# Forget gates of a linear-attention block as a bounded running product, and the last image's attention moved one chunk forward

## The chip, the cores and the metric

One core of one Trainium2 chip runs the whole program in one launch. The metric is the time of one execution on the device in microseconds (us). Before the change the median of three runs is 594.33 us (593.33 to 594.6).

## The reference, cut to what matters

Four images of 512 tokens go through a tokenizer (sines and cosines of six multiples of the input, times a weight matrix), a causal linear attention with forget gates, and a mixture of experts with a shared expert. A class token stands ahead of each image; it is the same for all, so it is computed once. The change touches the forget gates:

```
q = (elu(x @ Wq) + 1) * scale
k = elu(x @ Wk) + 1
v = x @ Wv
forget = sigmoid(x @ Wf + bf)
log_f = log(clip(forget, 1e-06, None))
log_f_cum = clip(cumsum(log_f, axis=1), -20, 20)
exp_neg, exp_pos = exp(-log_f_cum), exp(log_f_cum)
kv = k[..., :, None] * v[..., None, :]
Mstate = exp_pos[..., None] * cumsum(exp_neg[..., None] * kv, axis=1)
z = exp_pos * cumsum(exp_neg * k, axis=1)
h = einsum('blm,blmd->bld', q, Mstate) / (einsum('blm,blm->bl', q, z)[..., None] + 1e-06)
```

D = 192 features, M = 64 attention features, 512 tokens and the class token in a sequence. The kernel weighs q with exp_pos and k with exp_neg, and takes scores as one product of the two, masked by causality.

## The kernel before, in words

Every engine has its own program, written out by hand, and waits on semaphores. TensorE (PE) sets the pace. The program has three stages.

**Token stage** (to about 372 us). For each image b, `project(b, k)` for k = 0 to 8 multiplies nine groups of features into two PSUM banks, 48 PE instructions in the trace for each group. The features of a group come from GpSimd (POOL, L405), VectorE (DVE, `remainders`, L767 and L771) and ScalarE (ACT, `sines`, L476 and L479), in three slots. Between the groups PE does one attention step each of what is ready: beside image 0 the class token (called attention 0), beside image b the attention of image b - 1 (attention b, "a" in the code). The steps are `attn1` (transposes), `attn2` (gate, q, k and the first values), `attn2b` (the other values), `attn3` (scores), `attn5` (scores times values), `attn6`, `attn7` (output projection), `attn8`, `router`, `ranks`.

The gates in `attn2`: ACT takes exp(-x) into tile row R_S (`odds`, L513) and an exponential for q and k (L516). DVE cuts the odds (L805) and adds up q and k (L807). ACT takes ln(1 + odds) (`log_odds`, L521), DVE a running sum over the tokens (`running_sum`, a scan, L813) and a clip (L818), ACT the exponential of plus or minus that (`powers`, L526), DVE the product with q and k (`weigh_qk`, L824). A DMA that ACT's queue issues then moves k from the upper 64 partitions to the lower (`move_k`, L532), and PE's scores wait for it. On ACT sine, exponential, logarithm and SiLU each need their table loaded (ACT_TABLE_LOAD) when another was used before.

**Shared stage** (about 372 to 486 us). No token groups are left; PE fills the time around attention 4, that of the last image (B = 4), with chunks q = 0 to 18 of the shared expert. In chunk q it does `up(q)` (two halves of five matmuls, L1469 to L1473), the attention step that the table of numbers `Q_...` puts at q, and `down(q - 2)` (L1507). ACT does `silu(q)`, DVE `hidden(q)` (L1032), both with the same table for the attention steps behind them. ACT also rounds the expert weights (`expert_hi`, at `Q_HI`), DVE takes the remainders (`expert_lo`, L1056 and L1060, at `Q_LO`). Every sixth `down` begins a new image of the shared expert in the same PSUM banks, so `down(6)` waits for `finish(0)` and `down(12)` for `finish(1)` (L1040), which DVE does in chunk Q_X2 and in chunk Q_RK + 1. `places` is the arithmetic of the tokens' slots, after which GpSimd scatters the tokens.

**Expert stage** (from about 486 us). 39 tiles of gathered tokens go through the routed experts, then the class token's and five more chunks of the shared expert, the sums and the output.

```
Q_X1, Q_QKV, Q_V23, Q_RK3, Q_SCORES, Q_AV, Q_X2, Q_WO, Q_X3, Q_LG, Q_RK = 1, 2, 3, 4, 5, 6, 8, 9, 11, 12, 13
Q_HI = (5, 8, 11, 13)
Q_LO = (6, 9, 12, 14)
```

Of the kernel before, what the change touches and what calls it, by code (L numbers as in the profile page):

```python
# [11 lines left out]
ALU = mybir.AluOpType  # L12
ACT = mybir.ActivationFunctionType
AX_X = mybir.AxisListType.X

P = 128
B = 4
# [5 lines left out]
M = 64  # L23
# [33 lines left out]
MAX_ODDS = float(np.float32(1e6) - np.float32(1.0))  # L57
CLIP = 20.0
FAR = 1e30
# [8 lines left out]

Q_X1, Q_QKV, Q_V23, Q_RK3, Q_SCORES, Q_AV, Q_X2, Q_WO, Q_X3, Q_LG, Q_RK = 1, 2, 3, 4, 5, 6, 8, 9, 11, 12, 13
Q_HI = (5, 8, 11, 13)  # L70
Q_LO = (6, 9, 12, 14)

# [8 lines left out]
def build(nc, xT, wT, freqs, cls_tok, packed, wsa, wsb, wds, wea, web, wdea, wdeb, blank, slots, ydram, out):  # L81
    with ExitStack() as ctx:
        def sb(name, shape, dt=F32):
            return ctx.enter_context(nc.sbuf_tensor(name, shape, dt))
# [39 lines left out]
        f_col = sb("f_col", [P, NF + 3])  # L124
        qk_scale, p_sign = sb("qk_scale", [P, 1]), sb("p_sign", [P, 1])
        half_pi, warm = sb("half_pi", [P, 1]), sb("warm", [P, 1])
        one = sb("one", [P, 1])
# [23 lines left out]
        with ExitStack() as fourth:  # L151
# [9 lines left out]
        s_c = sb("s_c", [P, 1])  # L161
# [26 lines left out]

        R_E, R_PHI, R_S, R_P, R_C, R_QK, R_K = range(7)
        at = r[:, 0:4, :]  # L190
# [4 lines left out]
            h_ready ln_step xn_ready xpose1 xta_ready xtb_ready qk_psum f_psum v01_psum v23_psum v_ready  # L195
            e_ready ee_ready odds_ready oddsc_ready s_ready scan_ready c_ready p_ready phi_ready
            qk_ready k_in at_psum at_diag at_rest state_psum state_ready av_psum den_ready rden_ready hh_ready hn_ready
# [11 lines left out]
         h_ready, ln_step, xn_ready, xpose1, xta_ready, xtb_ready, qk_psum, f_psum, v01_psum, v23_psum, v_ready,  # L209
         e_ready, ee_ready, odds_ready, oddsc_ready, s_ready, scan_ready, c_ready, p_ready, phi_ready,  # L210
         qk_ready, k_in, at_psum, at_diag, at_rest, state_psum, state_ready, av_psum, den_ready, rden_ready, hh_ready, hn_ready,
# [14 lines left out]
        def width(a):  # L226

            cls = a == 0
            return (CLS, CLS, 1) if cls else (T, P, NT)
# [234 lines left out]
        def _(act):  # L464
# [52 lines left out]

            def log_odds(a):
                W, TP, nt = width(a)
                act.wait_ge(oddsc_ready, a + 1)  # L520
                act.activation(r[:, R_S, 0:W], r[:, R_S, 0:W], ACT.Ln, bias=one[:, :], scale=1.0).then_inc(s_ready, 1)  # L521

            def powers(a):
                W, TP, nt = width(a)
                act.wait_ge(c_ready, a + 1)
                act.activation(r[:, R_P, 0:W], r[:, R_C, 0:W], ACT.Exp, scale=p_sign[:, :]).then_inc(p_ready, 1)  # L526

            def move_k(a):
# [5 lines left out]
            def attn2(a):  # L534
                take_v(a, 0)
                odds(a)
                if a >= 1:
                    take_v(a, 1)
                log_odds(a)
                powers(a)  # L540
                move_k(a)
# [109 lines left out]
            for b in range(1, B):  # L651

                sines(b, 1)
                sines(b, 2)
                attn1(b)
                if b >= 2:
                    router(b - 1)
                sines(b, 3)
                odds(b)
                take_v(b, 0)  # L660
                sines(b, 4)
                take_v(b, 1)
                log_odds(b)
                powers(b)
                move_k(b)
                if b >= 2:
                    take_ranks(b - 1)
                sines(b, 5)
                attn3(b)
                sines(b, 6)  # L670
                sines(b, 7)
                attn6(b)
                sines(b, 8)
                attn8(b)
                if b + 1 < B:
                    sines(b + 1, 0)
                take_h(b)


            for q in range(NQB):  # L680
                silu(q)
                if q == Q_X1:
                    router(B - 1)
                    attn1(B)
                if q == Q_QKV:
                    odds(B)
                    take_v(B, 0)
                if q == Q_V23:
                    log_odds(B)
                    take_v(B, 1)  # L690
                    powers(B)
                    move_k(B)
                if q == Q_RK3:
                    take_ranks(B - 1)
                if q == Q_SCORES:
                    attn3(B)
                if q == Q_X2:
                    attn6(B)
                if q == Q_X3:
                    attn8(B)  # L700
                if q == Q_LG:
                    router(B)
                if q == Q_RK:
                    take_ranks(B)
                if q in Q_HI:
                    expert_hi(Q_HI.index(q))

# [16 lines left out]
        def _(dve):  # L724
# [77 lines left out]
            def clip_odds(a):  # L802
                W, TP, nt = width(a)
                dve.wait_ge(odds_ready, a + 1)
                dve.tensor_scalar(r[:, R_S, 0:W], r[:, R_S, 0:W], MAX_ODDS, None, ALU.min).then_inc(oddsc_ready, 1)  # L805
                dve.wait_ge(ee_ready, a + 1)
                dve.scalar_tensor_tensor(r[:, R_PHI, 0:W], ps[:, A2, 0:W], 0.0, r[:, R_E, 0:W],  # L807
                                         ALU.max, ALU.add).then_inc(phi_ready, 1)

            def running_sum(a):  # L810
                W, TP, nt = width(a)
                dve.wait_ge(s_ready, a + 1)
                dve.tensor_tensor_scan(r[:, R_C, 0:W], one[:, 0:1].to_broadcast([P, W]), r[:, R_S, 0:W],  # L813
                                       0.0 if a == 0 else s_c[:, 0:1], ALU.mult, ALU.add).then_inc(scan_ready, 1)
                dve.wait_ge(scan_ready, a + 1)
                if a == 0:
                    dve.tensor_copy(s_c[:, :], r[:, R_S, 0:1])
                dve.tensor_scalar(r[:, R_C, 0:W], r[:, R_C, 0:W], CLIP, -CLIP, ALU.min, ALU.max).then_inc(c_ready, 1)  # L818

# [7 lines left out]
            def attn2(a):  # L827
                negatives(a)
                clip_odds(a)
                running_sum(a)  # L830
                weigh_qk(a)
# [297 lines left out]
            dve.memset(qk_scale[M:P, :], 1.0)  # L1129
            dve.memset(p_sign[0:M, :], -1.0)  # L1130
            dve.memset(p_sign[M:P, :], 1.0)
            for t_ in (cnt, nbk, dold, nxt, emap):
# [36 lines left out]
            for b in range(1, B):  # L1169
# [14 lines left out]
                remainders(b, 4)  # L1184
                running_sum(b)
                weigh_qk(b)
# [20 lines left out]
            for q in range(NQB):  # L1207
# [10 lines left out]
                if q == Q_V23:  # L1218
                    running_sum(B)
                    weigh_qk(B)  # L1220
# [5 lines left out]
                if q == Q_AV:  # L1226
                    places(B - 1, [2])
                if q in Q_LO:
                    expert_lo(Q_LO.index(q))
# [549 lines left out]
```

## Time and profile before

| | |
|---|---|
| runs | 593.33, 594.6, 594.33 us; median 594.33 |
| profiled execution | 599.89 us, its span from first to last instruction 597.7 us |
| granted TensorE clock, mean | 0.975 of full |
| busy | PE 562.9 us (94%), DVE 363.3 (61%), ACT 249.8 (42%), POOL 173.8 (29%) |
| chain that ended last | PE 86%, DVE 8%, ACT 2%, DMA 1%, issue 1% |

Times in the trace count from the first instruction. A row of the timeline has start, duration, engine, line, operation, output and inputs, and in brackets how long the engine had been idle before it and who released it. A matmul in fp32 takes two PE instructions. The granted clock is 1.00 at TensorE's full clock (2.4 GHz) and 0.50 at the lower (1.2 GHz).

### The profile page before, as it was taken

Reading aid. Unit: us, or ns where it says so; the run is one execution under the profiler, and the core shown is the slowest. Engines: PE = TensorE matmul, PEld = TensorE weight load, DVE = VectorE, ACT = ScalarE, POOL = GpSimd, SP = SyncE. Lnnn points to the kernel's source line nnn. Section 1 sums busy time; section 2 is a strip of 40 time slices with the busy share of each in tenths; the row PEclk is TensorE's granted clock in tenths of the full one; section 3 lists DMA queues with packets and bytes.
Section 4 is the critical chain, followed back from the end, with each engine's and each line's share of the span. In section 5 each row is a group of like instructions: output and inputs, shape, how many; then the busy total and the mean of one; then the engine's idle time right before and its main releaser. Section 6 shows DMA issues by size and latency. Waiting matters only on the chain.

```text
span 597.7 us, 9035 instructions
## 1 busy us (share of the span) xinstructions
PE 562.9 (94%) x3247; PEld 516.8 (86%) x3247; DVE 363.3 (61%) x1041; ACT 249.8 (42%) x345; POOL 173.8 (29%) x200
## 2 busy tenths in 40 slices
PE   2999999999999999999999999999688699999996
PEld 2998999889999899999899999678577589999865
DVE  5636787443788627878537773646477436665536
ACT  2455364752423745224754242562223025455410
POOL 5412223131344114644311630005000504444410
PEclk9998999999999999999899999999798799999999
DMA  8900057000100001100000101401000651522173
GB/s 285 330 27 19 1 207 232 19 26 1 36 1 18 19 10 35 63 28 1 0 1 9 54 19 41 172 10 71 1 1 1 203 169 41 157 77 73 54 221 111
DMA packets 23648, 42.48 MB, mean 71 GB/s; under 512 B 2663, under 2 KB 15205, under 8 KB 23509
## 3 DMA queue, kind: packets, MB, share of 16 engines
q1 hardware_dynamic: 19568, 33.31, 17.5%
q0 software_dynamic: 3472, 8.07, 3.8%
q10 hardware_dynamic: 564, 0.53, 0.4%
q8 instruction: 27, 0.44, 0.3%
q14 instruction: 17, 0.13, 0.1%
HBM read 31.73 MB, written 14.79 MB: 78 GB/s over the span
## 4 chain that ended last, share of the span: by engine, by line
PE 86%; DVE 8%; ACT 2%; DMA 1%; issue 1%; POOL 0%; ACTq 0%; DVEq 0%
PE ps L1314 45%; PE ps L1507 5%; PE ps L1393 2%; PE ps L1559 2%; PE ps L1561 2%; PE ps L1469 2%; PE ps L1370 2%; PE ps L1471 2%; PE ps L1470 2%; PE ps L1472 2%; PE ps L1473 1%; PE ps L1342 1%; PE ps L1537 1%; PE ps L1538 1%; PE ps L1541 1%
## 5 line engine op out<-in xcount | busy, mean ns | idle before, releaser
L1314 PE MATMUL ps<-w_tok,feat 128*128 128x192 f32 x1728 | 293.4, 331 | 12.0 <-ACT feat L471 10.8
L1314 PEld LDWEIGHTS ps<-w_tok,feat 128*128 128x128 f32 x1728 | 285.4, 193 | 15.5 <-issue 15.1
L405 POOL TENSOR_SCALAR feat<-x,f_col 128x512 int32<-128x512 f32 x108 | 92.3, 870 | 211.6 <-PE ps L1314 204.7
L476 ACT ACTIVATE feat<-feat 128x1536 f32<-128x1536 f32 x35 | 51.9, 1484 | 116.6 <-DVE feat L771 114.0
L767 DVE SCALAR_TENSOR_TENSOR feat<-x,f_col,feat 128x512 f32<-128x512 f32 x105 | 76.6, 783 | 1.4 <-POOL feat L405 1.0
L479 ACT ACTIVATE feat<-feat,half_pi 128x1536 f32<-128x1536 f32 x36 | 56.2, 1560 | 0.0
L441 POOL DMA_INDIRECT ydram<-yr,xs x39 | 37.5, 962 | 59.1 <-DVE yr L1081 59.1
L1507 PE MATMUL ps<-w_down,hid_ring 128*128 128x192 f32 x192 | 39.9, 355 | 11.0 <-DVE H L1040 10.8
L1507 PEld LDWEIGHTS ps<-w_down,hid_ring 128*128 128x128 f32 x192 | 34.5, 205 | 14.0 <-issue 12.4
L1032 DVE TENSOR_TENSOR hid_ring<-s_ring,ps 128x512 f32<-128x512 f32 x24 | 16.5, 687 | 43.9 <-PE ps L1473 31.1
L435 POOL DMA_INDIRECT slots<-pay_a,posi x17 | 18.6, 1095 | 81.0 <-DVE posi L1008 77.6
L583 ACT ACTIVATE s_ring<-ps 128x512 f32<-128x512 f32 x24 | 14.4, 598 | 66.2 <-PE ps L1473 53.3
L771 DVE TENSOR_SCALAR feat<-feat 128x1536 int32<-128x1536 int32 x35 | 37.2, 1063 | 1.2
L605 ACT ACTIVATE xhr<-ps 128x256 fp32r<-128x256 f32 x39 | 15.0, 385 | 22.1 <-PE ps L1520 22.1
L1074 DVE TENSOR_TENSOR hidt<-sr,ps 128x192 f32<-128x192 f32 x39 | 13.8, 354 | 15.8 <-ACT sr L611 14.2
L1469 PE MATMUL ps<-X,wa_hi 128*128 128x512 f32 x48 | 23.1, 482 | 0.0
L1067 DVE TENSOR_TENSOR xlr<-ps,xhr 128x256 fp32r<-128x256 f32 x39 | 16.6, 424 | 10.6 <-ACT xhr L605 10.6
L1081 DVE TENSOR_SCALAR yr<-ps,xs 128x192 f32<-128x192 f32 x39 | 16.3, 418 | 8.5 <-PE ps L1561 6.1
L611 ACT ACTIVATE sr<-ps 128x192 f32<-128x192 f32 x39 | 12.9, 331 | 20.1 <-issue 15.4
L813 DVE TENSOR_TENSOR_SCAN r<-one,s_c,r 128x512 f32<-128x512 f32 x4 | 5.1, 1284 | 26.3 <-ACT r L521 26.3
L1471 PE MATMUL ps<-X,wa_hi 128*128 128x512 f32 x48 | 19.9, 415 | 0.0
L1559 PE MATMUL ps<-wd_ea,htr 128*128 x78 | 19.2, 328 | 0.7 <-DVE yr L1081 0.7
(276 smaller groups left out, 864.4 us busy)
## 6 DMA issues: line engine op xcount, KB each, us to landing
slots<-in_blank SPq DMA_DIRECT2D x1, 5031.0 KB, 19.2
x<-in_xT SPq DMA_DIRECT2D x16, 256.0 KB, 2.6
w_tok<-in_wT SPq DMA_DIRECT2D x7, 576.0 KB, 9.6
xs<-slots SPq DMA_DIRECT2D x5, 645.0 KB, 7.1
yin<-ydram SPq DMA_DIRECT2D x8, 384.0 KB, 6.8
raw_a<-in_wea SPq DMA_DIRECT2D x4, 384.0 KB, 5.6
raw_b<-in_web SPq DMA_DIRECT2D x4, 384.0 KB, 6.2
w_tok<-in_wT SPq DMA_DIRECT2D x4, 288.0 KB, 8.9
```

Of the source, the lines that this page charges most:

```text
L405: ins = pool.tensor_scalar(feat[:, k % SLOTS, i, :].bitcast(I32), x[:, x_block(k), :], f_col[:, fi:fi + 1], 1.0, ALU.mult, ALU.mult)
L435: pool.indirect_dma_start(slots, bass.IndirectOffsetOnAxis(ap=idx, axis=0), (pay_a[a % 2], pay_b)[c][0:TP, t, :], None).then_inc(scat, 16)
L441: pool.indirect_dma_start(ydram, bass.IndirectOffsetOnAxis(ap=idx, axis=0), yr[:, s % NYR, :], None).then_inc(yscat[s % NYR], 16)
L476: act.activation(feat[:, k % SLOTS, 0:3, :], feat[:, k % SLOTS, 0:3, :], ACT.Sin, scale=TWO_PI).then_inc(sin_ready, 1)
L479: act.activation(feat[:, k % SLOTS, 3:6, :], feat[:, k % SLOTS, 3:6, :], ACT.Sin, bias=half_pi[:, :], scale=-TWO_PI).then_inc(sin_ready, 1)
L767: ins = dve.scalar_tensor_tensor(feat[:, s, i, :], x[:, x_block(k), :], f_col[:, fi:fi + 1], feat[:, s, i, :].bitcast(I32), ALU.mult, ALU. ...
L771: dve.tensor_scalar(feat[:, s, 3:6, :].bitcast(I32), feat[:, s, 0:3, :].bitcast(I32), 0x7FFFFFFF, None, ALU.bitwise_and).then_inc(r_ready, 1)
L1314: ins = pe.matmul(ps[:, TOK[a % 2][t // 2], (t % 2) * D:(t % 2 + 1) * D], feat[:, k % SLOTS, i, t * P:(t + 1) * P], w_tok[:, k, i, :], sta ...
L1469: pe.matmul(o, wa_hi[:, c, i, :], xh, start=True, stop=False)
L1471: pe.matmul(o, wa_hi[:, c, i, :], xl, start=False, stop=False)
L1507: ins = pe.matmul(ps[:, DN0 + t // 2, (t % 2) * D:(t % 2 + 1) * D], hid_ring[:, q % 3, t * P:(t + 1) * P], w_down[:, c, :], start=(c == 0 ...
L1559: pe.matmul(o, htr[:, s % 2, 0:P], wd_ea[:, bass.ds(e, 1), :].rearrange("p e n -> p (e n)"), start=True, stop=False)
```

## The change

1. `clip_odds` adds 1 to the cut odds in the same DVE instruction, so that R_S holds 1 / forget. `log_odds` and `powers` are removed from ACT in all five attentions. `running_product` multiplies the values up over the tokens in one scan, with a minimum against e^20 at each step; k's half is used as it is, and q's half (64 partitions) is inverted by a DVE reciprocal in place of the clip.
2. In the shared stage the steps of attention 4 from the ranks of attention 3 on, and with them `Q_HI` and `Q_LO`, come one chunk earlier.

```diff
-Q_X1, Q_QKV, Q_V23, Q_RK3, Q_SCORES, Q_AV, Q_X2, Q_WO, Q_X3, Q_LG, Q_RK = 1, 2, 3, 4, 5, 6, 8, 9, 11, 12, 13
-Q_HI = (5, 8, 11, 13)
-Q_LO = (6, 9, 12, 14)
+Q_X1, Q_QKV, Q_V23, Q_RK3, Q_SCORES, Q_AV, Q_X2, Q_WO, Q_X3, Q_LG, Q_RK = 1, 2, 3, 3, 4, 5, 7, 8, 10, 11, 12
+Q_HI = (4, 7, 10, 12)
+Q_LO = (5, 8, 11, 13)
...
-            def log_odds(a):
-                W, TP, nt = width(a)
-                act.wait_ge(oddsc_ready, a + 1)
-                act.activation(r[:, R_S, 0:W], r[:, R_S, 0:W], ACT.Ln, bias=one[:, :], scale=1.0).then_inc(s_ready, 1)
-
-            def powers(a):
-                W, TP, nt = width(a)
-                act.wait_ge(c_ready, a + 1)
-                act.activation(r[:, R_P, 0:W], r[:, R_C, 0:W], ACT.Exp, scale=p_sign[:, :]).then_inc(p_ready, 1)
...
-                dve.tensor_scalar(r[:, R_S, 0:W], r[:, R_S, 0:W], MAX_ODDS, None, ALU.min).then_inc(oddsc_ready, 1)
+                dve.tensor_scalar(r[:, R_S, 0:W], r[:, R_S, 0:W], MAX_ODDS, 1.0, ALU.min, ALU.add).then_inc(oddsc_ready, 1)
...
-            def running_sum(a):
-                W, TP, nt = width(a)
-                dve.wait_ge(s_ready, a + 1)
-                dve.tensor_tensor_scan(r[:, R_C, 0:W], one[:, 0:1].to_broadcast([P, W]), r[:, R_S, 0:W],
-                                       0.0 if a == 0 else s_c[:, 0:1], ALU.mult, ALU.add).then_inc(scan_ready, 1)
-                dve.wait_ge(scan_ready, a + 1)
+            def running_product(a):
+
+                W, TP, nt = width(a)
+                dve.wait_ge(oddsc_ready, a + 1)
+                dve.tensor_tensor_scan(r[:, R_P, 0:W], r[:, R_S, 0:W], most[:, 0:1].to_broadcast([P, W]),
+                                       1.0 if a == 0 else s_c[:, 0:1], ALU.mult, ALU.min).then_inc(scan_ready, 1)
                 if a == 0:
                     dve.tensor_copy(s_c[:, :], r[:, R_S, 0:1])
-                dve.tensor_scalar(r[:, R_C, 0:W], r[:, R_C, 0:W], CLIP, -CLIP, ALU.min, ALU.max).then_inc(c_ready, 1)
+                dve.wait_ge(scan_ready, a + 1)
+                dve.reciprocal(r[0:M, R_P, 0:W], r[0:M, R_P, 0:W]).then_inc(p_ready, 1)
```

The calls of `log_odds` and `powers` go, those of `running_sum` become `running_product`, and one constant tile takes the place of another.

**ACT, chunks 2 to 4 of the shared stage**, from the gate's exponential of attention 4 (L513) to the rank copy (L576 before, L564 now); `s_ring` is SiLU's output. Before:

```order
L513 ACTIVATE r<-ps,pack 128x512
L516 ACTIVATE r<-r 128x512
L504 ACTIVATE v<-ps 128x2x192
L583 ACT_TABLE_LOAD
L583 ACTIVATE s_ring<-ps 128x512
L521 ACT_TABLE_LOAD
L521 ACTIVATE r<-r,one 128x512
L504 ACTIVATE v<-ps 128x2x192
L526 ACT_TABLE_LOAD
L526 ACTIVATE r<-r,p_sign 128x512
L532 DMA r<-r 64x512
L583 ACT_TABLE_LOAD
```

With the change:

```order
L513 ACTIVATE r<-ps,pack 128x512
L516 ACTIVATE r<-r 128x512
L504 ACTIVATE v<-ps 128x2x192
L571 ACT_TABLE_LOAD
L571 ACTIVATE s_ring<-ps 128x512
L504 ACTIVATE v<-ps 128x2x192
L522 DMA r<-r 64x512
L564 ACTIVATE rks<-ps 128x40
L571 ACTIVATE s_ring<-ps 128x512
```

The logarithm, the second exponential and three table loads are gone, and the rank copy stands ahead of the next SiLU.

**DVE, chunks 3 and 4**, between two `hidden`s (L1032 before, L1017 now). Before:

```order
L1032 TENSOR_TENSOR hid_ring<-s_ring,ps 128x512
L813 SCALAR_TENSOR_TENSOR r<-one,s_c,r 128x512
L818 TENSOR_SCALAR r<-r 128x512
L824 SCALAR_TENSOR_TENSOR r<-r,qk_scale 128x512
L1032 TENSOR_TENSOR hid_ring<-s_ring,ps 128x512
L985 TENSOR_TENSOR aft<-cnt,rks 128x8
```

With the change:

```order
L1017 TENSOR_TENSOR hid_ring<-s_ring,ps 128x512
L798 SCALAR_TENSOR_TENSOR r<-r,s_c,most 128x512
L803 RECIPROCAL r<-r 64x512
L809 SCALAR_TENSOR_TENSOR r<-r,qk_scale 128x512
L970 TENSOR_TENSOR aft<-cnt,rks 128x8
```

The scan is listed as SCALAR_TENSOR_TENSOR. A reciprocal of 64 x 512 takes the clip's place, and the slot arithmetic of attention 3 now comes ahead of `hidden(4)`.

**PE, chunk 4**, from the second half of `up(4)` to `down(2)`. Before (ranks of attention 3, and the scores one chunk later):

```order
L1472 MATMUL ps<-X,wb 128x512
L1473 MATMUL ps<-X,wb 128x512
L1456 MATMUL ps<-oh,causal_bf 128x32
L1459 MATMUL ps<-oh,ones_bf 128x24
L1459 MATMUL ps<-oh,ones_bf 128x16
L1459 MATMUL ps<-oh,ones_bf 128x8
L1463 MATMUL ps<-oh,ones_bf 128x8 x4
L1507 MATMUL ps<-w_down,hid_ring 128x192 x4
```

With the change:

```order
L1456 MATMUL ps<-X,wb 128x512
L1457 MATMUL ps<-X,wb 128x512
L1354 MATMUL ps<-r 128x512
L1354 MATMUL ps<-r 128x384
L1354 MATMUL ps<-r 128x256
L1354 MATMUL ps<-r 128x128
L1491 MATMUL ps<-w_down,hid_ring 128x192 x4
```

The scores (L1370 before, L1354 now) stand directly behind `up(4)`.

## Rows read from the trace of the kernel before

**Rows 1.** The page: busy time of three engines, share of the span, instructions.

```profile
PE 562.9 (94%) x3247; PEld 516.8 (86%) x3247; DVE 363.3 (61%) x1041; ACT 249.8 (42%) x345; POOL 173.8 (29%) x200
```

**Rows 2.** Waits of PE: total us, times, longest us.

```profile
PE ps L1507 <- DVE H L1040: 10.8, 3, 7.9
...
PE ps L1402 <- DVE xn L753: 3.0, 1, 3.0
```

**Rows 3.** Timeline, 34 to 70 us: the class token's gates, and what follows.

```profile
40.51 0.17 DVE L805 TENSOR_SCALAR r<-r 128x2 f32<-128x2 f32 x1 [2.66 <-ACT r L513]
40.59 1.28 ACT L521 ACT_TABLE_LOAD   x1
...
43.96 2.07 DVE L767 SCALAR_TENSOR_TENSOR feat<-x,f_col,feat 128x512 f32<-128x512 f32 x3
...
46.41 0.19 PE L1370 MATMUL ps<-r 64*2 64x2 f32 x2
...
47.06 1.48 ACT L476 ACTIVATE feat<-feat 128x1536 f32<-128x1536 f32 x1 [1.18 <-DVE feat L771]
...
48.68 9.72 PE L1314 MATMUL ps<-w_tok,feat 128*128 128x192 f32 x48 [1.07 <-ACT feat L476]
...
58.51 8.07 PE L1314 MATMUL ps<-w_tok,feat 128*128 128x192 f32 x48
```

**Rows 4.** PE by stretch: us, length and busy (instructions), granted clock, DMA share, GB/s.

```profile
50.00:52.00 2.00, 2.00 (x8) 0.50 0.00 0
192.00:194.00 2.00, 2.00 (x18) 1.00 0.00 0
...
288.00:290.00 2.00, 2.00 (x8) 0.50 0.00 0
428.00:430.00 2.00, 2.00 (x7) 0.50 0.00 0
```

**Rows 5.** DVE's groups by shape: busy us, mean ns of one.

```profile
L813 DVE TENSOR_TENSOR_SCAN r<-one,s_c,r 128x512 f32<-128x512 f32 x4 | 5.1, 1284 | 26.3 <-ACT r L521 26.3
...
L818 DVE TENSOR_SCALAR r<-r 128x512 f32<-128x512 f32 x4 | 1.7, 428 | 0.1
...
L959 DVE RECIPROCAL iz<-iz 128x8 f32<-128x8 f32 x4 | 0.8, 203 | 0.1
...
L859 DVE RECIPROCAL rden<-den 128x4 f32<-128x4 f32 x4 | 0.7, 178 | 0.1
```

**Rows 6.** Timeline, 100 to 135 us: attention 1's gates.

```profile
116.30 0.96 DVE L771 TENSOR_SCALAR feat<-feat 128x1536 int32<-128x1536 int32 x1
...
128.28 0.75 DVE L824 SCALAR_TENSOR_TENSOR r<-r,qk_scale 128x512 f32<-128x512 f32 x1 [0.79 <-ACT r L526]
...
131.33 2.42 PE L1370 MATMUL ps<-r 64*128 64x512 f32 x8 [0.19 <-DMA r<-r]
```

**Rows 7.** Timeline, 386 to 418 us: `hidden(3)`, the end of `up(4)`, the scores, two `down`s.

```profile
392.44 0.69 DVE L1032 TENSOR_TENSOR hid_ring<-s_ring,ps 128x512 f32<-128x512 f32 x1 [3.23 <-PE ps L1473]
...
397.57 0.19 PE L1456 MATMUL ps<-oh,causal_bf 128*128 128x32 bf16 x1
...
401.59 2.42 PE L1370 MATMUL ps<-r 64*128 64x512 f32 x8
...
412.65 1.46 PE L1507 MATMUL ps<-w_down,hid_ring 128*128 128x192 f32 x8
...
416.28 1.46 PE L1507 MATMUL ps<-w_down,hid_ring 128*128 128x192 f32 x8
```

**Rows 8.** Timeline, 416 to 474 us: `hidden(7)`, `down(6)`, `attn7`, `down(12)`.

```profile
418.80 0.69 DVE L1032 TENSOR_TENSOR hid_ring<-s_ring,ps 128x512 f32<-128x512 f32 x1 [2.49 <-PE ps L1507]
...
426.59 2.90 PE L1507 MATMUL ps<-w_down,hid_ring 128*128 128x192 f32 x8 [2.41 <-DVE H L1040]
...
432.43 1.46 PE L1415 MATMUL ps<-pack,xt_a 128*128 128x192 f32 x8
...
468.54 2.90 PE L1507 MATMUL ps<-w_down,hid_ring 128*128 128x192 f32 x8 [7.92 <-DVE H L1040]
```

More of the change, by code:

```diff
@@ L57 @@
 MAX_ODDS = float(np.float32(1e6) - np.float32(1.0))
-CLIP = 20.0
+MAX_GROWTH = float(np.exp(np.float32(20.0)))
 FAR = 1e30
@@ L124, in build @@
         f_col = sb("f_col", [P, NF + 3])
-        qk_scale, p_sign = sb("qk_scale", [P, 1]), sb("p_sign", [P, 1])
+        qk_scale, most = sb("qk_scale", [P, 1]), sb("most", [P, 1])
         half_pi, warm = sb("half_pi", [P, 1]), sb("warm", [P, 1])
@@ L187, in build @@
         ps = ctx.enter_context(nc.psum_tensor("ps", [P, 8, 512], F32))
-        R_E, R_PHI, R_S, R_P, R_C, R_QK, R_K = range(7)
+        R_E, R_PHI, R_S, R_P, R_QK, R_K = 0, 1, 2, 3, 5, 6
         at = r[:, 0:4, :]
@@ L195, in build @@
             h_ready ln_step xn_ready xpose1 xta_ready xtb_ready qk_psum f_psum v01_psum v23_psum v_ready
-            e_ready ee_ready odds_ready oddsc_ready s_ready scan_ready c_ready p_ready phi_ready
+            e_ready ee_ready odds_ready oddsc_ready scan_ready p_ready phi_ready
             qk_ready k_in at_psum at_diag at_rest state_psum state_ready av_psum den_ready rden_ready hh_ready hn_ready
@@ L209, in build @@
          h_ready, ln_step, xn_ready, xpose1, xta_ready, xtb_ready, qk_psum, f_psum, v01_psum, v23_psum, v_ready,
-         e_ready, ee_ready, odds_ready, oddsc_ready, s_ready, scan_ready, c_ready, p_ready, phi_ready,
+         e_ready, ee_ready, odds_ready, oddsc_ready, scan_ready, p_ready, phi_ready,
          qk_ready, k_in, at_psum, at_diag, at_rest, state_psum, state_ready, av_psum, den_ready, rden_ready, hh_ready, hn_ready,
@@ L538, in attn2 @@
                     take_v(a, 1)
-                log_odds(a)
-                powers(a)
                 move_k(a)
@@ L662, in _ @@
                 take_v(b, 1)
-                log_odds(b)
-                powers(b)
                 move_k(b)
@@ L688, in _ @@
                 if q == Q_V23:
-                    log_odds(B)
                     take_v(B, 1)
-                    powers(B)
                     move_k(B)
@@ L829, in attn2 @@
                 clip_odds(a)
-                running_sum(a)
+                running_product(a)
                 weigh_qk(a)
@@ L1129, in _ @@
             dve.memset(qk_scale[M:P, :], 1.0)
-            dve.memset(p_sign[0:M, :], -1.0)
-            dve.memset(p_sign[M:P, :], 1.0)
+            dve.memset(most[:, :], MAX_GROWTH)
             for t_ in (cnt, nbk, dold, nxt, emap):
@@ L1184, in _ @@
                 remainders(b, 4)
-                running_sum(b)
+                running_product(b)
                 weigh_qk(b)
@@ L1218, in _ @@
                 if q == Q_V23:
-                    running_sum(B)
+                    running_product(B)
                     weigh_qk(B)
```

## Prediction

> **What bounds the kernel now.** I read the page first: PE is busy for 94% of the span, so only what PE waits for, or what slows it, can pay [rows 1]. The list of PE's waits comes next. It is short, and nearly all of it lies in the shared stage: 10.8 us in three waits for DVE's `finish` (L1040), of which one takes 7.9, and 3.0 us for the normed heads before `attn6` [rows 2]. The timeline then shows two more places. In image 0, PE stands for 1.07 us before `project(0, 4)`, because the sines of that group are late; and that group then takes 9.72 us where the one behind it takes 8.07 [rows 3]. The windows say why: the granted clock is 0.50 there (1.2 GHz) after some 2 us in which PE had only the class token's tiny matmuls and the wait. A similar poor stretch before 192 us left the clock at 1.00 and one before 288 us did not [rows 4]. So a poor stretch costs up to 1.7 us more, but not each time, and I count such a cost at half. In the shared stage PE's own work up to `down(12)` is the same with the change as before, only in another order; the time of `down(12)` therefore changes by waits and clock alone.
>
> **1. The class token's gates (image 0).** Before, DVE has cut the odds at 40.51 us, then ACT loads a table, takes the logarithm, loads another, takes the exponential; only behind that can DVE start the remainders of group 4, at 43.96. They end 3.1 us later, the sine starts at 47.06, PE at 48.68, while PE could have gone on from about 46.4, where its scores of the class token start [rows 3]. Now DVE goes straight on: from 40.51, six instructions on two columns or one, at about 0.17 each (the cut's own row), end at 41.5. The remainders end at 44.6, the sine at 46.1. PE does its small class-token steps from 46.41 (about 1 us, as before) and goes on at 47.4, with no wait for the sine. That is 1.3 us, less 0.2 for group 5, whose sines then come just in time. The slow stretch costs 9.72 - 8.07 = 1.65; with less than half of the poor time left it may go, at half 0.85. Term: 1.3 - 0.2 + 0.9 = **2.0**; ends 1.1 and 2.8.
>
> **2. Attentions 1 to 3.** PE waits for the moved k once, for 0.19 us [rows 6]. Now the scan needs nothing from ACT: it may start when the remainders of group 4 end, at 116.30 + 0.96 = 117.3. With the scan's 1.28, a reciprocal (below) of 3.35 and 0.75 for the weighing, k goes out at 122.7 instead of 129.0. Remainders behind it wait for GpSimd anyway. DVE's extra 2.9 us for each image lie in idle time. Term: **0.2**; ends 0 and 0.2.
>
> **3. The reciprocal, the one unknown price.** Before shows none of 512 columns. Of 8 columns it takes 203 ns, of 4 columns 178 [rows 5]: 25 ns for 4 more, 6.25 ns each, so 203 + 504 x 6.25 = 3.35 us. The lower end is the clip in whose place it stands, 0.43 us. The upper end takes all of the 203 ns as rate: 25.4 x 512 = 13.0 us. I take 3.35, since both rows are of the same instruction and only their difference is rate. The scan's rate is no guide, and its price stays at 1.28, since its two operations are again one after the other. The other edits of DVE (plus 1 in the cut) cost nothing, as the instruction is there already.
> The Trainium skill, VectorE: DVE Perf Modes, section "First, the fixed hardware budget", says that the reciprocal is an iterative divide with a repeat count of 8, on an engine of 0.96 GHz. If that means eight cycles for each column, a reciprocal of 512 takes an estimated 4.3 us plus overhead, some 1 us more than my price, and the sum below would be 5.9 in place of 6.9; no trace here shows a wide one.
>
> **4. The scores of attention 4, one chunk earlier.** `up(4)` ends at 397.57 before; with the ranks ahead of it now, at 397.8. The scores then stand next, and they need k. `hidden(3)` ends at 392.44 + 0.69 = 393.1, the scan at 394.4, the reciprocal at 397.8, the weighing at 398.5. From the end of the weighing to PE's scores the DMA takes 131.33 - 129.03 = 2.3 us [rows 6]. PE starts the scores at 400.8: **a new wait of 3.0 us** stands where none was. Behind ACT's DMA issue, which waits for the weighing, stand the rank copy and `silu(4)`; `up(5)`'s second half wants that SiLU only at about 405, so it holds nobody. Before, the scores started at 401.59 [rows 7]. Term: 401.6 - 400.8 = **0.8**. For every microsecond that the reciprocal takes more or less it falls or rises by one, down to a price near 0.7, where PE itself is the limit. Less a slow clock that the new wait may bring, up to 1.7, at half: **-0.8**.
>
> **5. From the scores to `attn6`.** The same work as before, except that DVE stood for 2.49 us ahead of `hidden(7)` [rows 8], although `up(7)` was done (`down(5)` behind it starts at 416.28 [rows 7]). I find no rule in the program that holds it. If it belongs to this one execution, or stays in both, nothing is gained; if the new order avoids it, 2.45. Half: **1.2**. The 3.0 us wait before `attn6` [rows 2] is the end of this same chain, and shrinks only with it.
>
> **6. `finish(0)`.** Before, `attn6` and `down(6)` are in one chunk, so DVE has to do `hidden(8)`, its half of `attn6` and four instructions of `finish(0)` while PE waits 2.41 us. Now `attn6` is in chunk 7 and `down(6)` in chunk 8, behind `up(8)` and `attn7`, some 6 us of PE's work later: the wait goes. It lies between `attn6` and `attn7`, hence on the attention's own chain. Term: **2.4**. From `down(6)` to `attn7` before takes 432.43 - 426.59 = 5.84 us at a clock of 0.50 [rows 4, 8], where the same work takes 416.28 - 412.65 = 3.63 [rows 7]; if the slow stretch goes with the waits, 2.2 more. Half: **1.1**. The next wait, before `attn8`, is DVE's layernorm behind `attn7` and stays.
>
> **7. `finish(1)`.** It ends 13.6 us behind the router's last DVE step, through ez, `hidden`, `gates`, `places`, `expert_lo`: unchanged, so `down(12)` shifts by terms 4 to 6. PE's wait of 7.92 [rows 8] falls to about 6.4, since PE has more chunk work to do meanwhile. Then the same chunks and experts follow; the tokens' scatter moves with the places, and the expert tiles, loaded from 475 us on and used at 486, keep their slack. Term 0.
>
> **Sum:** 2.0 + 0.2 + 0.8 - 0.8 + 1.2 + 2.4 + 1.1 = 6.9 us. It is made against the profiled execution, 599.89 us (span 597.7), which is 5.6 above the median: 593.0. I take the same difference from the median of the runs: 594.3 - 6.9 = **587.4 us**. What a measurement can tell from no change is about 0.2%, 1.2 us.
>
> **Rivals.**
> *A, the reciprocal is cheap* (up to 0.7 us, as the clip's row). For it: DVE's other work of this width takes 0.4 to 0.8. Against it: the two reciprocal rows. The new wait falls below 0.5 and takes no clock with it: 6.9 + 2.6 + 0.8 = 10.3, so 584.0. Chance 0.12.
> *B, the last image's chain is as long as before*: the time saved at `finish(0)` comes back at a later step of the same chain, in the end before `down(12)`. For it: PE waits for DVE in four places there. Against it: the 2.41 us end no DVE work that the chain needs. Only terms 1 and 2 stay, 2.2: 592.1. Chance 0.10.
> *C, slower: the reciprocal is dear.* In each of attentions 1 to 3, PE reaches its scores at 131.1 and k is there at 117.3 + 1.28 + 0.75 + 2.3 = 121.7 plus the reciprocal, so from 9.4 us on PE waits in all three as well [rows 6]; the last image pays from the start. The gain is used up at 9.6 us; at the upper end of 13.0 it is 6.9 - 9.65 - 3 x 3.6 = -13.5, so 607.9 us. Only the reading of 203 ns as pure rate speaks for it. Chance 0.05.
>
> **How the numbers follow.** The forecast's mechanism has 0.73, A 0.12, B 0.10, C 0.05. With every half at its bad end the forecast gives 6.9 - 0.9 - 0.9 - 1.2 - 1.1 = 2.8 (591.5), and with all at the good end 6.9 + 0.8 + 0.8 + 1.2 + 1.1 = 10.8 (583.5). The range from 583.0 to 592.3 takes in these, A's time and B's; C, the outermost of A and the part of B that keeps nothing stay out, some 2 in 10. Faster by over 0.2%: the forecast, A and half to two thirds of B, 0.90; within 0.2%: the rest of B, 0.05; slower: C, 0.05.
>
> **What would show it.** Right: no table load for a logarithm; `project(0, 4)` starts near 47.4; L803 near 3.35 us; PE waits some 3 us for the DMA of k before the scores (L1354); no wait for L1025 at the seventh `down`, and one of 6 to 7 us at the thirteenth. Wrong: a reciprocal far from 3.35; a wait of PE in `attn7` or `attn8` that is longer than before; a slow clock in stretches that were fast.

## The result, and the profile after

The changed kernel takes 590.85 us (median of 4 runs, 590.25 to 591.1), the kernel before 594.41 beside it: ratio 0.9942, 95% interval 0.9925 to 0.996, so 2.4 to 4.5 us faster. I had forecast 587.4, that is 6.9 us faster. The direction is right and the time lies inside the range, but the gain is half of what I worked out. The profiled execution of after took 590.25 us, span 588.2, mean granted clock 0.983 (before 0.975). Its busy line, beside [rows 1]:

```profile
PE 561.2 (95%) x3247; PEld 514.5 (87%) x3247; DVE 375.4 (64%) x1040; ACT 225.6 (38%) x321; POOL 172.7 (29%) x200
```

What PE waited for, in total, how often, and the longest, beside [rows 2]:

```profile
PE ps L1298 <- ACT feat L471: 9.2, 1, 9.2
PE ps L1491 <- DVE H L1025: 4.7, 2, 4.3
PE ps L1354 <- DMA r<-r: 2.9, 1, 2.9
PE ps L1411 <- DVE pay_a L740: 1.6, 1, 1.6
...
PE ps L1386 <- DVE xn L737: 0.8, 1, 0.8
```

The first is the start of the kernel. The waits for `finish` fell from 10.8 us to 4.7; in their place stands the wait for k that I had forecast at 3.0 us. DVE's groups by shape, beside [rows 5]:

```profile
L803 DVE RECIPROCAL r<-r 64x512 f32<-64x512 f32 x4 | 13.4, 3345 | 0.1
L798 DVE TENSOR_TENSOR_SCAN r<-r,s_c,most 128x512 f32<-128x512 f32 x4 | 5.1, 1277 | 0.0
L809 DVE SCALAR_TENSOR_TENSOR r<-r,qk_scale 128x512 f32<-128x512 f32 x4 | 4.1, 1024 | 0.1
```

The reciprocal takes 3345 ns where I had put 3.35 us. Now the timeline of image 0, where [rows 3] showed the wait for the sines and the slow group:

```profile
40.41 0.16 DVE L803 RECIPROCAL r<-r 64x2 f32<-64x2 f32 x1
...
41.03 2.07 DVE L751 SCALAR_TENSOR_TENSOR feat<-x,f_col,feat 128x512 f32<-128x512 f32 x3
...
44.12 1.48 ACT L476 ACTIVATE feat<-feat 128x1536 f32<-128x1536 f32 x1 [1.17 <-DVE feat L755]
...
45.90 0.19 PE L1354 MATMUL ps<-r 64*2 64x2 f32 x2
...
46.90 8.07 PE L1298 MATMUL ps<-w_tok,feat 128*128 128x192 f32 x48
...
55.58 1.70 PE L1298 MATMUL ps<-w_tok,feat 128*128 128x192 f32 x9 [0.43 <-ACT feat L476]
```

`project(0, 4)` starts 1.00 us behind the class token's scores instead of 2.27, and takes 8.07 us instead of 9.72. Then the shared stage, PE's timeline:

```profile
391.33 0.40 PE L1457 MATMUL ps<-X,wb 128*128 128x512 f32 x1
394.60 4.63 PE L1354 MATMUL ps<-r 64*128 64x512 f32 x8 [2.88 <-DMA r<-r]
399.16 2.93 PE L1491 MATMUL ps<-w_down,hid_ring 128*128 128x192 f32 x8
...
405.42 1.57 PE L1373 MATMUL ps<-state,r 64*128 64x193 f32 x8
...
418.47 0.66 PE L1386 MATMUL ps<-pack,xn 128*128 128x128 f32 x4 [0.76 <-DVE xn L737]
...
459.14 2.90 PE L1491 MATMUL ps<-w_down,hid_ring 128*128 128x192 f32 x8 [4.25 <-DVE H L1025]
```

Behind the wait of 2.88 us the scores take 4.63 us where [rows 7] show 2.42, and `down(2)` takes 2.93 us where it takes 1.55 in the kernel before. PE's windows (start and end, length and busy, instructions, granted clock, DMA share, GB/s) say why:

```profile
392.00:394.00 2.00, 0.00 (x0) 1.00 0.28 60
394.00:396.00 2.00, 1.40 (x2) 0.52 0.05 13
...
402.00:404.00 2.00, 2.00 (x6) 0.50 0.00 0
404.00:406.00 2.00, 2.00 (x9) 0.92 0.39 136
```

The clock fell to 0.50 (1.2 GHz) during the wait, at 394.1 us, and stood there to 404.3 us. This is the first suspect: the new wait costs its clock as well as its length.

### The profile page after: what moved, and what is told of

It is laid out like the page before. It is cut to its first block, busy times and chain, and to the rows that moved or that the text cites. A ratio compares the mean times of both kernels' runs of the same rounds, so it can differ in the third digit from the quotient of the medians.

```text
span 588.2 us, 9010 instructions
## 1 busy us (share of the span) xinstructions
PE 561.2 (95%) x3247; PEld 514.5 (87%) x3247; DVE 375.4 (64%) x1040; ACT 225.6 (38%) x321; POOL 172.7 (29%) x200
## 3 DMA queue, kind: packets, MB, share of 16 engines
q0 software_dynamic: 3472, 8.07, 3.9%
## 4 chain that ended last, share of the span: by engine, by line
PE 86%; DVE 10%; issue 1%; DMA 1%; ACT 1%; POOL 0%; ACTq 0%; DVEq 0%
PE ps L1298 46%; PE ps L1491 4%; PE ps L1377 2%; PE ps L1543 2%; PE ps L1545 2%; PE ps L1354 2%; PE ps L1453 1%; PE ps L1454 1%; PE ps L1455 1%; PE ps L1456 1%; PE ps L1457 1%; PE ps L1521 1%; PE ps L1525 1%; PE ps L1522 1%; PE ps L1523 1%
## 5 line engine op out<-in xcount | busy, mean ns | idle before, releaser
L1017 DVE TENSOR_TENSOR hid_ring<-s_ring,ps 128x512 f32<-128x512 f32 x24 | 16.5, 686 | 34.1 <-PE ps L1457 33.4
L1454 PE MATMUL ps<-X,wa_lo 128*128 128x512 f32 x48 | 19.4, 405 | 0.0
```

The lines of the kernel that those rows point to most:

```text
L1454: pe.matmul(o, wa_lo[:, c, i, :], xh, start=False, stop=False)
```

## The experiments

All were run with the kernel before on the same chip. "Ratio" is against that kernel, with its 95% interval; 0.1% is 0.6 us. Line numbers in a profile are those of that kernel's own code, so they differ by a few. A row at the end of a view is cut off there: it shows only the first part of its instructions.

**1. What belongs to the profiled execution of before?** It was 5.6 us above its median, so I profiled the same kernel again, twice.

> The kernel before, once more. Theory one (the profiled execution was like the others): the rows return: DVE stands some 2.5 us ahead of hidden(7), project(0, 4) takes 9.7 us, PE runs at 0.50 between down(6) and attn7, span near 597. Theory two (part of what I counted belonged to that one execution, which was 5.5 us above the median): the span is near 592, and at least one of the three (the 2.49 us stand, the 1.65 us of project(0, 4), the 2.2 us behind down(6)) is gone.

> The kernel before, a third profile. If the slow clock of project(0, 4) and of the stretch behind down(6) belong to the kernel, both are there again (9.7 us, and 4.2 us or more from attn6 to attn7 over the changed kernel's 4.55); DVE's stand of 2.49 us ahead of hidden(7), seen in the first profile alone, is not.

Measured: 596.35 and 594.27 us (spans 594.2 and 592.1). The last, `before_third`, stands at the median (594.3) and is the right partner for after. PE in it:

```profile
48.89 9.72 PE L1314 MATMUL ps<-w_tok,feat 128*128 128x192 f32 x48 [1.06 <-ACT feat L476]
...
398.80 2.42 PE L1370 MATMUL ps<-r 64*128 64x512 f32 x8
...
404.98 1.57 PE L1389 MATMUL ps<-state,r 64*128 64x193 f32 x8
...
418.13 0.66 PE L1402 MATMUL ps<-pack,xn 128*128 128x128 f32 x4 [0.85 <-DVE xn L753]
421.63 2.53 PE L1507 MATMUL ps<-w_down,hid_ring 128*128 128x192 f32 x8 [2.41 <-DVE H L1040]
...
426.95 1.46 PE L1415 MATMUL ps<-pack,xt_a 128*128 128x192 f32 x8
```

The slow `project(0, 4)` is there in all three profiles of before (9.72 or 9.73 us), and so is the slow stretch behind `down(6)`: from `attn6` to `attn7` 9.34, 8.81 and 8.82 us, against 4.55 in after. DVE's stand of 2.49 us ahead of `hidden(7)` [rows 8] is in the first alone; in the others PE waits 0.85 us for `attn6`, not 3.0. So theory two holds for that stand, theory one for the rest. The other excess of the first two profiles is slow clock in the token stage: from PE's first matmul to the transposes of attention 4 they take 368.0 and 368.1 us, the third 365.8, with the same code. The two have stretches at 0.50 near 288 and 373 us, the third has neither.

Step by step on PE, third profile of before against after (us):

| stretch | before | after | gained |
|---|---|---|---|
| to PE's first matmul (loads) | 10.03 | 9.22 | 0.81 |
| to the transposes of attention 4 | 365.80 | 363.20 | 2.60 |
| to its scores | 22.97 | 22.18 | 0.79 |
| to `attn5` | 6.18 | 10.82 | -4.64 |
| to `attn6` | 13.15 | 13.05 | 0.10 |
| to `attn7` | 8.82 | 4.55 | 4.27 |
| to `attn8` | 12.06 | 12.06 | 0 |
| to `down(12)` | 24.05 | 24.06 | -0.01 |
| to the first expert tile | 17.50 | 17.44 | 0.06 |
| to the end | 111.54 | 111.62 | -0.08 |

The sum is 3.9, the difference of the spans. The first row is a matter of when the loads landed, so 3.1 us are left for the change. The second row holds only as far as this pair of profiles goes: neither has a slow stretch in the token stage but the one at `project(0, 4)`, which before has and after has not. Other profiles of kernels with the new gates take 363.0 to 365.9 us there.

**2. Each half of the change alone.** `gates_alone` is the new gates with the old `Q_...` lines, `order_alone` the old gates with the new ones:

```diff
-Q_X1, Q_QKV, Q_V23, Q_RK3, Q_SCORES, Q_AV, Q_X2, Q_WO, Q_X3, Q_LG, Q_RK = 1, 2, 3, 3, 4, 5, 7, 8, 10, 11, 12
+Q_X1, Q_QKV, Q_V23, Q_RK3, Q_SCORES, Q_AV, Q_X2, Q_WO, Q_X3, Q_LG, Q_RK = 1, 2, 3, 4, 5, 6, 8, 9, 11, 12, 13
```

> The new gates, the old table of chunks. By my sum only terms 1 and 2 stay, and the reciprocal lies beside PE's chunk work because the scores stand one chunk later: 2.2 us under before, 592.2, with no wait of PE for k in the last image. Rival (the reciprocal hurts by itself in the last image, through hidden, places or the tiles behind it): no gain or a loss, 594 to 597. If slow clock at project(0, 4) was an accident of the profiled execution, the gain is 1.3 us only (593.1).

> The old gates (logarithm and exponential), the new table. In before's profile the weighed k is ready 6.2 us of PE's time later than it would be in the new order, at about 391.1 on after's time scale, where the reciprocal has it at 392.3; so PE waits some 1.7 us for k instead of 2.9. Theory one (my terms 4 to 6, a slow clock costs 0.8 on average): 2.1 - 0.8 + 1.2 + 3.5 = 6.0 us under before, 588.4. Theory two (PE's clock falls after each such wait and costs 4 to 5 us from the scores on, in every execution): 1 to 2 us under before, 592.4 to 593.4, and the profile shows scores of 4.6 us where before shows 2.4.

Measured: `gates_alone` 594.07 us, ratio 0.9985 (0.9965 to 1.0006). `order_alone` 592.08 us, ratio 0.9946 (0.9924 to 0.9968), which is 3.2 us under before (1.9 to 4.5): more than theory two's 1 to 2, and far from my sum's 6.0. The gain of `gates_alone`, 0.9 us, is not clear of noise. The two halves add up to 4.1 us, where the whole change gave 3.4 here and 2.6 in its second set of runs (experiment 3), so most of what can be measured comes from the order. PE in `order_alone`, timeline and windows:

```profile
398.16 4.19 PE L1370 MATMUL ps<-r 64*128 64x512 f32 x8 [1.64 <-DMA r<-r]
402.28 2.93 PE L1507 MATMUL ps<-w_down,hid_ring 128*128 128x192 f32 x8
```

```profile
396.00:398.00 2.00, 0.53 (x3) 1.00 0.33 74
398.00:400.00 2.00, 1.84 (x3) 0.66 0.00 0
400.00:402.00 2.00, 2.00 (x6) 0.50 0.00 0
```

The same pattern without any reciprocal: PE waits for k, then the scores and `down(2)` run at 0.50, and from the scores to `attn5` it takes 9.48 us in place of 6.17. So it comes with the new order of the chunks; the new gates only lengthen the wait. It is 1.64 us here, as expected: in the last image the logarithm has k ready 1.2 us sooner than the reciprocal. The gates alone bring most of their gain in image 0 (`project(0, 4)` 0.99 us behind the scores, 8.07 us long), and from the class token's scores to `project(0, 7)` its profile takes 26.93 us, after 26.95, before 29.39: 2.5 us less. By the runs it is only 0.9 us. Its profile has slow stretches of clock at 285 and 370 us, where the third one of before has none.

**3. Is it the clock, and is it the wait?** Two edits of after that leave its other work alone, and after itself once more. `down_first`: PE does `down(2)` ahead of the scores.

```diff
                 if q == Q_SCORES:
+                    down(q - 2)
                     attn3(B)
...
-                if q >= 2:
+                if q >= 2 and q != Q_SCORES:
                     down(q - 2)
```

`fill_wait`: PE does matmuls whose result is overwritten unread, where it waited. The wait for the values moves ahead of them.

```diff
+                pe.wait_ge(v_ready, a + 1)
+                if a == B:
+                    for _ in range(5):
+                        pe.matmul(ps[:, A0, 0:W], wff_a, xt_a[:, 0:W], start=True, stop=True)
                 pe.wait_ge(k_in, 16 * (a + 1))
                 pe.wait_ge(qk_ready, a + 1)
-                pe.wait_ge(v_ready, a + 1)
```

> The changed kernel, but in chunk 4 PE does down(2) ahead of the scores, in the time in which it waits for k (2.9 us, of which down(2) fills 1.5). Theory one (a slow clock behind the wait costs 0.8 on average): 1.5 to 2.3 us under the changed kernel, 588.6 to 589.4. Theory two (the wait of 2.9 us lowers the clock each time, and costs 4.65 us between the scores and attn5): with 1.4 us of wait left the clock stays at 1.00, and the kernel is 4 to 6 us under the changed one, 585 to 587. If the clock falls all the same, 1.5 us under: 589.4.

> The changed kernel with five more matmuls of 512 columns (0.53 us each) on PE between up(4) and the scores of attention 4, in the 2.9 us in which PE waits for k; their result is overwritten unread. k arrives no sooner, so the scores start when they did, 22.2 us after the first transposes of attention 4; only PE's idleness is gone. Theory two (the idle time lowers the clock, and that costs 4.65 us on top of the wait): the scores take 2.4 us again, 6.2 us from the scores to attn5 instead of 10.8, and 4 to 5 us under the changed kernel, 586 to 587. Rival (the clock falls because of the scores themselves, which use 64 of 128 rows, or for a cause that has nothing to do with the wait): 10.8 us again and no change, 591.

> The changed kernel once more, with more runs. Theory two (the wait for k lowers the clock each time): the scores take 4.6 us at a granted clock of 0.50 again, down(2) 2.9. Theory one (it was a draw of that execution): the scores take 2.4 us. The time: 3 to 4 us under before.

Measured: `down_first` 588.36 us, ratio 0.9893 (0.9864 to 0.9923); `fill_wait` 588.46, ratio 0.9879 (0.9847 to 0.9911); `after_again` 591.28, ratio 0.9957 (0.9935 to 0.998), its scores 4.63 us and 10.86 us to `attn5` once more. PE in `fill_wait`, timeline and windows:

```profile
393.46 4.45 PE L1350 MATMUL ps<-xt_a,pack 128*128 128x512 f32 x10
397.84 2.42 PE L1357 MATMUL ps<-r 64*128 64x512 f32 x8
...
404.03 1.24 PE L1376 MATMUL ps<-state,r 64*128 64x193 f32 x6
```

```profile
396.00:398.00 2.00, 2.00 (x6) 1.00 0.04 9
...
402.00:404.00 2.00, 2.00 (x9) 1.00 0.00 0
```

This settles it. The kernel does more work than after, its scores start later (the five matmuls take 4.45 us, not the 2.65 I had meant: each is two instructions of 0.44; so the scores stand 23.53 us behind the transposes instead of 22.18), and it is still 2.4 us or more faster, because the clock stays at 1.00 and `attn5` follows the scores after 6.19 us. So it is PE's idleness that lowers the clock there, and the rival that the scores' 64 rows do it by themselves falls. The runs agree: the mean granted clock is 0.989 in all six of `fill_wait` and 0.977 to 0.984 in all sixteen of after.

In `down_first` the clock also holds, though PE waits 1.58 us:

```profile
393.23 1.46 PE L1491 MATMUL ps<-w_down,hid_ring 128*128 128x192 f32 x8
...
396.27 2.42 PE L1354 MATMUL ps<-r 64*128 64x512 f32 x8 [1.58 <-DMA r<-r]
```

`order_alone` waited 1.64 us, hardly more, and fell. The length of the wait alone does not decide; which other thing does (what stands ahead of the wait, or its moment) stays open. `half_more` was meant to ask that:

> product_first, in which PE does not wait for k, with a second reciprocal of 256 columns into a tile that nobody reads, ahead of the real one in attention 4: k is some 1.6 us later, and PE waits about 1.4 us. If the clock goes by the length of the wait alone, it stays at 1.00, as in down_first (1.58 us of wait), and the time is 1.4 us over product_first, 586.7. If it goes by what surrounds the wait (order_alone waited 1.64 us, with the scores behind it, and fell to 0.50), the scores or what is behind them run at 0.50 and the time is 4 to 5 us over product_first, 589.5 to 590.

It does not answer. `product_first` (below) has k ready before PE wants it (the DMA lands at 393.89 us, the scores start at 394.91), which I had overlooked, so the wait came out at 0.57 us, with the clock at full and 585.16 us in all, ratio 0.9827 (0.9792 to 0.9863), no slower than `product_first`.

**4. Take the wait away, and put it back.** `product_first` moves two calls of DVE's program from chunk 3 to chunk 2, ahead of `hidden(3)`:

```diff
                 if q == Q_QKV:
                     negatives(B)
                     clip_odds(B)
-                if q == Q_V23:
                     running_product(B)
                     weigh_qk(B)
```

`double_reciprocal` is that kernel with a second reciprocal of 512 columns ahead of the real one, into a tile that nobody reads. `short_reciprocal` is after with a reciprocal of 8 columns in attentions 1 to 4; it leaves out the inversion of all other columns of q's half, so its output is not that of the reference.

> The changed kernel, but in the last image DVE does the running product, the reciprocal and the weighing ahead of hidden(3) instead of behind it; DVE stands idle there for 3.2 us while PE does up(3). k is then ready some 3 us sooner and PE's wait of 2.9 us for it goes. Theory one (the wait costs its own length and a slow clock 0.8 on average): 3 to 4 us under the changed kernel, 587. Theory two (the wait costs its length, and 4.65 us of slow clock behind it each time): attention 4 takes 39 to 40 us from its first transposes to attn6, where the changed kernel takes 46.05 and down_first 41.1; 5 to 7 us under the changed kernel, 584 to 586. Rival (hidden(3), now 2.1 us later, holds up(5) or down(3)): no gain over down_first.

> The changed kernel with the reciprocal of 8 columns instead of 512 in attentions 1 to 4; the decay of the other queries is not inverted (this leaves out part of the computation). It asks what the 3.35 us of the reciprocal cost. If they cost only through PE's wait for k in the last image: the same as product_first within 1 us (584 to 586 by theory two, 587 by theory one). If they also cost in images 1 to 3, by holding the remainders behind them: over 1.5 us under product_first. If the reciprocal lay beside PE's work all along: no change to the changed kernel.

> product_first with a second reciprocal of all 512 columns into a tile that nobody reads, ahead of the real one in attention 4: k is 3.35 us later and PE's wait comes back, some 3 us. Theory one: 3.0 + 0.8 over product_first, 589. Theory two: 3.0 + 4.65 over it, 592.9, and 10.8 us from the scores to attn5; a change of 3.35 us on DVE then costs 7.6 us.

Measured: `product_first` 585.26 us, ratio 0.9845 (0.9808 to 0.9881); `short_reciprocal` 584.98, ratio 0.9843 (0.9804 to 0.9882); `double_reciprocal` 592.93, ratio 0.9964 (0.9935 to 0.9994). DVE and then PE in `product_first`:

```profile
386.18 1.27 DVE L798 TENSOR_TENSOR_SCAN r<-r,s_c,most 128x512 f32<-128x512 f32 x1
387.49 3.35 DVE L803 RECIPROCAL r<-r 64x512 f32<-64x512 f32 x1
390.87 0.75 DVE L809 SCALAR_TENSOR_TENSOR r<-r,qk_scale 128x512 f32<-128x512 f32 x1
391.54 0.68 DVE L1017 TENSOR_TENSOR hid_ring<-s_ring,ps 128x512 f32<-128x512 f32 x1
```

```profile
394.91 2.42 PE L1353 MATMUL ps<-r 64*128 64x512 f32 x8
...
401.08 1.08 PE L1372 MATMUL ps<-state,r 64*128 64x193 f32 x5
```

The whole stretch from the transposes of attention 4 to `attn6` takes 38.4 us, as theory two had it (39 to 40); after needs 46.05 there, before 42.3, `down_first` 41.1. By the ratios the kernel is 9.2 us under before, so some 6 under after. With the reciprocal cut to 0.20 us nothing more is won: its 3.35 us cost only through the wait that they cause, and lie in DVE's idle time in images 1 to 3. The second reciprocal brings the wait back (2.16 us, not the 3 expected, by the same slack of 1.0 us) and the clock's fall with it:

```profile
395.63 4.15 PE L1355 MATMUL ps<-r 64*128 64x512 f32 x8 [2.16 <-DMA r<-r]
...
405.12 1.08 PE L1374 MATMUL ps<-state,r 64*128 64x193 f32 x5
```

9.49 us from the scores to `attn5`, and 44.65 in place of 38.4 from the transposes to `attn6`. So 3.35 us more on DVE cost 6.3 us there and 7.1 us by the ratios.

**5. The longest wait that is left.** `both_sooner` is `product_first` with `finish(1)` straight behind `hidden(13)` on DVE, ahead of `expert_lo(3)` and the last part of `places`:

```diff
+                if q == Q_RK + 1:
+                    finish(1)
                 if q in Q_LO:
                     expert_lo(Q_LO.index(q))
...
                     places(B, [2])
-                    finish(1)
```

> product_first, and in chunk 13 DVE does finish(1) straight behind hidden(13), ahead of the split of the experts' weights (1.9 us) and the last part of places (2.1 us). PE's wait for finish(1) (4.3 us in the changed kernel, 5.9 in down_first, longer by what product_first gains) falls by 3.9 us, since nothing in finish(1) needs either of them. Expected 3 to 4 us under product_first, 581 to 583, and a shorter slow stretch behind the wait. Rival (the map of the experts is then late and PE waits for it at the first tile): no gain.

Measured: 580.48 us (577.92 to 580.8), ratio 0.9755 (0.9716 to 0.9794), some 14 us faster than before. PE's wait at `down(12)`, in `product_first` and here:

```profile
454.88 1.44 PE L1490 MATMUL ps<-w_down,hid_ring 128*128 128x192 f32 x5 [4.31 <-DVE H L1025]
```

```profile
450.80 1.38 PE L1491 MATMUL ps<-w_down,hid_ring 128*128 128x192 f32 x7 [0.34 <-DVE H L1025]
```

3.97 us of wait go, and the slow stretch behind it goes too: from `down(12)` to the first expert tile 15.88 us instead of 17.51. The first tile does not wait for the map of the experts, so the rival falls. This is the fastest version, and faster than both kernels.

## Why the prediction was right and wrong

By its own steps, with the forecast of each and what the table of experiment 1 has in its place:

- **Steps 1 and 2** (2.2 forecast, 2.6 in the table). Right in mechanism; the size is right in the traces of image 0 (29.39 us before, 26.95 after and 26.93 in `gates_alone`, experiment 2), but the runs do not confirm it. The wait for the sines went (2.27 us to 1.00), group 5 gave back 0.43 where I had 0.2, and the slow clock of `project(0, 4)`, which I counted at half, was in all profiles of before and in none of a kernel with the new gates. `order_alone`, with the old gates, ran that group in 8.04 us, though, so it is frequent and not certain. The runs of `gates_alone` give 0.9 us, at most 2.1 and perhaps nothing, and slow clock at 285 and 370 us of its profile is the only difference I see; why that comes there in some executions stays open.
- **Step 3**, the price from two small rows, was exact: 3.35 forecast, 3.345 measured. The Trainium skill, VectorE: DVE Perf Modes, section "First, the fixed hardware budget", led to an estimate of 4.3 us; here one column more costs (3345 - 203) / 504 = 6.2 ns, which is 6.0 cycles of its 0.96 GHz. My reading of the repeat count as eight cycles for each column does not hold in this trace.
- **Step 4 failed, in the term for the clock.** Its first half was right: a wait of 3.0 us forecast, 2.88 measured, scores 0.8 us earlier, 0.79 measured. But I wrote "Less a slow clock that the new wait may bring, up to 1.7, at half: -0.8". It brought 4.6 to 4.7 us in the two profiles of after, and 3.3 in `order_alone` and in `double_reciprocal`. The price was taken from `project(0, 4)`, where the clock was low for 3.4 us; at this wait it was low for 10.2. Nothing in before showed a wait ahead of the scores, and I took the mildest of its slow stretches as the upper end, although my own step 6 had one that cost 2.2. The error here is 3.8 us, as much as the whole difference between 6.9 and 3.1. That the two agree so well is luck: the errors of the other steps (0.4 us too little in 1 and 2, 1.1 too much in 5, 0.8 too little in 6) cancel.
- **Step 5** (1.2 forecast, 0.1 measured). The stand of DVE belonged to that one execution; `attn6` waits 0.85 us in the other profiles of before and 0.76 in after. A half of something that I could not explain was too much.
- **Step 6** (3.5 forecast, 4.27 measured). Right, and the half was too cautious: the slow clock behind `down(6)` is in every profile of before.
- **Step 7** (0 forecast, 0 measured). `down(12)` starts 24.05 us behind `attn8` in both. Its wait, which I put at 6.4 us, is 4.25. I had counted some 1.5 us more chunk work for PE ahead of it; it is a whole chunk, since `attn8` moved one chunk forward and `down(12)` did not. PE's work between the two grew from 24.05 - 7.90 = 16.15 us to 24.06 - 4.25 = 19.81, by 3.66, and a chunk takes 3.63 [rows 7]. A slow stretch lies in this span in both kernels (the `down` at 445.72 us in the third profile of before takes 2.73 us, that at 441.80 in after 2.84). It costs nothing there: the second profile of before does not have it, waits 9.53 us instead of 7.90, and takes the same 24.04 us from `attn8` to `down(12)`.

The rivals: A (cheap reciprocal) and C (dear) fall with its price. B, that the chain of the last image stays as long, came close in number (592.1 against 590.85), but not in mechanism: the time saved at `finish(0)` did not come back later, it had been lost before, at the scores. The case that came true, the new wait with a slow clock dearer than 1.7 us behind it, was none of my rivals; I had folded the clock into step 4.

## What to carry to other kernels

A new wait of the engine that sets the pace has two prices, its length and the clock behind it; here 2.9 us of wait cost 4.6 us more, and filling it with useless matmuls paid. The second price does not follow the first: waits of 1.64 and 2.16 us ahead of the scores cost 3.3 us more, one of 1.58 us behind `down(2)` cost nothing, and 4.3 us ahead of `down(12)` cost 1.6 (17.51 us to the first expert tile, 15.88 without it). No run here shows what sets it. So look in the order of the instructions for what could stand ahead of the wait: moving two calls of DVE's program into its idle time was worth more than the whole change. And before costing anything from one profile, take a second: a stretch that one execution alone shows is no term of a sum.

## What the hardware showed that I had not expected

- The low clock that came with a wait of 2.88 us lasted 10.2 us in after (394.1 to 404.3 us), and hit matmuls of every kind: the scores 4.63 us instead of 2.42, `down(2)` 2.93 instead of 1.55. With the waits of 1.64 and 2.16 us (`order_alone`, `double_reciprocal`) it lasted 6.8 us, with 4.25 us ahead of `down(12)` in after only 3.4.
- In the token stage, with no wait of PE near, whole stretches at half clock come in some profiles and not in others with the same code up to there, also of one kernel (experiment 1). PE alone, in `product_first` and then in after:

```profile
284.00:288.00 4.00, 4.00 (x17) 0.59 0.00 0
370.00:374.00 4.00, 4.00 (x13) 0.57 1.02 359
```

```profile
284.00:288.00 4.00, 4.00 (x27) 1.00 0.00 0
370.00:374.00 4.00, 4.00 (x22) 1.00 1.01 366
```

From PE's first matmul to attention 4 the one takes 365.9 us, the other 363.2. The runs of the kernel before spread from 591.1 to 598.3 us, and their mean clock goes with the time: 0.986 in those near 591 us, 0.976 in those of 597 and 598. So such stretches probably make most of the spread, and nothing below about 1 us could be settled here.

- The weighing of q and k (L809) takes 1.11 or 1.12 us in attentions 1 to 3 and 0.75 in attention 4, where before it took 0.75 in all four (L824); in the first three its place in time is another, and which neighbour slows it was not tried.
